# Windowed attention: score products of both heads ahead of their masks, and the next batch's products between scores and masks

## The reference, cut to what matters

```
L, D = 256, 256 in the block's own setup; here x is 1 x 1024 x 256
NQ, NKV, HD, SW = 32, 8, 64, 64;  QM = 4
q, k, v = split(layernorm(x) @ W_qkv);  q, k = rope(q), rope(k)
attn = einsum('bqhmd,bkhd->bhmqk', q, k) * sm_scale
mask = (q_pos >= k_pos) & (q_pos < k_pos + SW)
attn = where(mask, -inf, attn)
w = softmax(concat([attn, sink]))[..., :-1]
out = einsum('bhmqk,bkhd->bqhmd', w, v)
y = out @ W_out
```

## Time and profile before

| | |
|---|---|
| Runs of the kernel | 2770.3, 2771.74, 2782.01 us; median 2771.74 |
| Profiled execution | 2764.51 us, of which the span of the trace is 2762.8 |
| TensorE busy, whole span | 2515.4 us (91%) in 14474 products |
| VectorE, ScalarE, GpSimd busy | 1625.1 (59%), 1259.8 (46%), 1290.9 us (47%) |
| Second attention, from its first score tile | 634 to 1331 us of the span, 16 batches |
| In it, TensorE busy | 679.89 of 697.00 us |
| Mask products (L1836) | 288, 71.5 us busy, mean 248 ns |

### The profile page before, as it was taken

The page is one execution under the profiler, slowest core; times in us unless marked ns, Lnnn a source line. Parts: engine busy times, 40 slices in busy tenths (PEclk is TensorE's granted clock), DMA queues, the critical chain, the costliest instruction groups (busy, mean ns, idle before and its releaser), DMA issues. The chain is left out here.

```text
span 2762.8 us, 40694 instructions
## 1 busy us (share of the span) xinstructions
PE 2515.4 (91%) x14474; PEld 1675.7 (61%) x14474; DVE 1625.1 (59%) x2163; ACT 1259.8 (46%) x2174; POOL 1290.9 (47%) x1130
## 2 busy tenths in 40 slices
PE   6887999888999999999878878889999988998798
PEld 4443777654444444444564436678888877776676
DVE  4663555576766766665336543477777745555655
ACT  4464333464555555555434652256655643333322
POOL 4100344486888888888630002255454533442243
PEclk9798999998999999999976989899999999999899
DMA  1000111121101111010000001100010001110111
GB/s 59 1 2 11 39 46 46 48 80 39 39 16 39 31 31 39 16 35 1 25 26 1 1 1 49 47 20 28 20 32 20 20 5 42 46 46 21 31 41 43
DMA packets 39710, 81.63 MB, mean 30 GB/s; under 512 B 7553, under 2 KB 21121, under 8 KB 39041
## 3 DMA queue, kind: packets, MB, share of 16 engines
q1 hardware_dynamic: 39264, 79.41, 10.2%
q10 hardware_dynamic: 288, 0.13, 0.0%
HBM read 59.07 MB, written 2.62 MB: 22 GB/s over the span
## 5 line engine op out<-in xcount | busy, mean ns | idle before, releaser
L2019 DVE TENSOR_REDUCE a1h_mseg<-bank 128x2 f32<-128x1024 f32 x256 | 302.6, 1221 | 187.2 <-PE bank L1776 173.2
L63 POOL TENSOR_TENSOR f_wh<-f_raw,ones_r 128x768 fp32r<-128x768 f32 (+1 forms) x74 | 112.5, 1520 | 534.9 <-PE bank L462 360.0
L1953 ACT ACTIVATE a1h_prob<-bank 128x512 f32<-128x512 f32 x366 | 206.1, 598 | 165.6 <-PE bank L1836 83.8
L1756 POOL TENSOR_TENSOR a_qk<-a_qk,a1h_prob 128x512 f32<-128x512 f32 x186 | 238.9, 1318 | 50.8 <-ACT a1h_prob L1953 50.8
L451 PE MATMUL bank<-x_norm_h,f_wh 128*128 128x512 f32 x592 | 243.1, 411 | 6.7 <-PEq L3249 2.5
L451 PE MATMUL bank<-x_norm_l,f_wh 128*128 128x512 f32 x592 | 237.5, 401 | 0.0
L451 PE MATMUL bank<-x_norm_h,f_wl 128*128 128x512 f32 x592 | 237.0, 400 | 0.0
L658 DVE SCALAR_TENSOR_TENSOR f_tf<-bank,f_bias,f_sg 128x512 f32<-128x512 f32 x148 | 110.9, 750 | 187.2 <-PE bank L451 180.8
L542 ACT ACTIVATE f_hhi<-f_hf 128x512 fp32r<-128x512 f32 x124 | 78.3, 632 | 275.6 <-DVE f_hf L666 275.6
L1834 PE MATMUL bank<-a1h_ql,a1h_k 128*128 128x512 f32 x512 | 203.2, 397 | 0.0
L1849 PE MATMUL bank<-a1h_prob,a_v 128*64 128x512 f32 x732 | 179.9, 604 | 0.0
(11 more groups left out here) (597 smaller groups left out, 6277.1 us busy)
## 6 DMA issues: line engine op xcount, KB each, us to landing
f_raw<-in_l_w_dram SPq DMA_DIRECT2D x66, 385.0 KB, 3.0
a1h_st_q<-a_qk SPq DMA_DIRECT2D x128, 128.0 KB, 2.4
l2a_qkraw<-in_l2a_wqk_dram SPq DMA_DIRECT2D x32, 128.0 KB, 2.1
l2a_vraw<-in_l2a_wvg_dram SPq DMA_DIRECT2D x8, 512.0 KB, 3.7
f_raw<-in_l_w_dram SPq DMA_DIRECT2D x8, 449.0 KB, 3.3
a_qk<-l_keys SPq DMA_DIRECT2D x24, 128.0 KB, 2.7
a1p_raw<-in_l1a_w_dram SPq DMA_DIRECT2D x20, 128.0 KB, 2.1
a_qk<-in_l1a_wo_dram SPq DMA_DIRECT2D x16, 128.0 KB, 2.1
```

Source lines behind the costliest of these rows:

```text
L63: return pool.tensor_tensor(dst, src, one.to_broadcast(list(src.shape)), ALU.mult)
L1756: pool.tensor_tensor(out, first, slot_of[t % NP], ALU.add).then_inc(sum_done, 1)
L1953: act.activation(slot_of[t % NP], core.bank[2 + t % 3][:, :], ACT.Exp, scale=scale).then_inc(p_ready, 1)
L2019: dve.tensor_reduce(mseg[:, :, qb, s], spare(("A", n, k))[:, :, :], AX.X, ALU.max).then_inc(a_read, 1)
```

## The change

Only TensorE's order within a visit changes. `scores(n, i)` now does both heads of a step: the first head's two products, the second head's two, and without the masks. The masks of both heads follow in a function of their own, `mask_scores`. In the second step of a visit, where the next batch has segments in that visit and batch 0 isn't in its first three visits, the products of the two segments (`maxima`) go between that step's scores and its masks; the segments' masks come after the scores' masks. Everywhere else the masks follow the scores of their step at once. Every wait and every semaphore stays with its instruction, and no other engine's program is changed.

```diff
-            def scores(n, i, a):
+            def scores(n, i):
...
+                for a in range(PER):
...
+                    pe.matmul(bank[:, :], kn[:, G % 2, a, keys], QA[n % 2][:, a, half(h)], start=True, stop=False)
+                    mm = pe.matmul(bank[:, :], k1[:, a, keys], ql[:, n % 2, a, half(h)], start=False, stop=lo >= hi)
+                    if lo >= hi:
+                        mm.then_inc(s_ready, 1)
+            def mask_scores(n, i):
+
+                h, kb = TILES[i]
+                lo, hi = max(kb * P, h * HALF), min(kb * P + BAND, (h + 1) * HALF)
+                for a in range(PER if lo < hi else 0):
+                    bank = core.bank[2 + tile(n, i, a) % 3]
+                    pe.matmul(bank[:, lo - h * HALF:hi - h * HALF], core.ident_b[:, :],
+                              mk[:, 0, lo - kb * P:hi - kb * P], start=False, stop=True).then_inc(s_ready, 1)
...
                         for i in (2 * j, 2 * j + 1):
-                            scores(n, i, 0)
-                            scores(n, i, 1)
+                            scores(n, i)
+                            if i == 2 * j or (n == 0 and j < 3) or j == 7:
+                                mask_scores(n, i)
+                            else:
+                                for k in pairs[0:2]:
+                                    maxima(n + 1, k)
+                                mask_scores(n, i)
+                                for k in pairs[0:2]:
+                                    mask_maxima(n + 1, k)
...
-                        visit(n + 1, pairs[0:2])
+                        if (n == 0 and j < 3) or j == 7:
+                            visit(n + 1, pairs[0:2])
```

More of the change, by code:

```diff
@@ L1831, in scores @@
                 keys = slice(kb * P, (kb + 1) * P)
                 lo, hi = max(kb * P, h * HALF), min(kb * P + BAND, (h + 1) * HALF)
[L1833 to L1837, removed]
@@ L1838, in scores @@
-                mm.then_inc(s_ready, 1)
+                for a in range(PER):
+                    t = tile(n, i, a)
+                    bank = core.bank[2 + t % 3]
+                    if i == 0:
+                        pe.wait_ge(m_rows, rows_of(n) + a + 1)
+                        pe.wait_ge(q_lo, PER * n + a + 1)
+                    if n == 0 and i == TB:
+                        pe.wait_ge(m_rows, rows_of(n, "N") + a + 1)
+                    if i == 0 and a == 0:
+                        if n == 0:
+                            pe.wait_ge(k1_ones, PER)
+                        if n % 4 == 0:
+                            pe.wait_ge(k1_act, G + 1)
+                            pe.wait_ge(k1_dve, G + 1)
+                    if t >= 3:
+                        pe.wait_ge(p_ready, t - 2)
+                    pe.matmul(bank[:, :], kn[:, G % 2, a, keys], QA[n % 2][:, a, half(h)], start=True, stop=False)
+                    mm = pe.matmul(bank[:, :], k1[:, a, keys], ql[:, n % 2, a, half(h)], start=False, stop=lo >= hi)
+                    if lo >= hi:
+                        mm.then_inc(s_ready, 1)
```

## The result

The changed kernel is slower: median 2808.87 us of six runs (2799.57 to 2813.89), against 2771.02 for the kernel before (2761.31 to 2782.01, six runs). The ratio is 1.0121, 95% interval 1.0099 to 1.0144; of 2771 us that is 33.5 us, 27 to 40. The two medians lie 37.9 us apart, which is inside that interval.

The account below looks back on a forecast made before the run. TensorE's start-to-start product chain was taken as the bound. Visit costs over all batches summed to 36.1 us, less 1 given back: net +35 us, on the lowest run shown (2770.3) 2805 us; 8-in-10 range 2780 to 2820.

Parts of the forecast that it names:

- What bounds: Windowed attention: TensorE, busy 679.89 of 697.0 us, is near its limit; start-to-start distances count, not the weight path's 79.8 us idle.
- The new wait: Before the fourth K of masked visits: first tile's late mask, then its exponential, must finish; 0.77 us from mask end.
- fourth K: Fourth first score product (L1833) of a visit; in visit 6 forecast 2.06 us behind the first, against 1.79 before.
- Second mask behind the first: Score mask (L1836) directly behind another: starts 0.08 us later, bounds 0.03 and 0.24.
- M to m: From the next batch's row-maxima products (L1776) to the score masks (L1836): 0.67 us, type and tile shape both changing.
- The visits: Added time per masked visit: visits 1 and 6 +0.55 us, 0 +0.69, 5 +0.23, 7 +0.34; 2.36 a batch.
- V of visit 6: Start of visit 6's value products (L1849), counted from its first score product: forecast 3.85 us, against 3.30 before.
- The unmasked visits: Visits 2, 3, 4, order unchanged: said to run already at the exponential chain's limit, fourth K at 1.51 us.
- Given back: Masks now covering TensorE's waits for VectorE's reductions: under 1.9 us, taken as 1 us off the sum.
- (a): Rival: the wait before the fourth K doesn't bite, only tile shape changes cost; +12 us, 2783; chance 0.15.
- (b): Rival: no wait, mixing types was the cost, shape changes free between bf16 products; 8 us less, 2763; chance 0.12.
- (c): Rival: both added shape changes cost a full tail and load, 0.35 instead of 0.10; 29 us more, 2834; chance 0.07.

Follow-up runs that it names:

- grouped_only: Changed kernel, but the next batch's products stay behind all score masks; ratio to the kernel before 1.0102, stage 718.2 us (+22.0).
- odd_grouped: Kernel before, with both heads' masks together only in a visit's second step (not visit 5), next batch's products behind them; ratio 0.9999, stage 692.8 us (-3.4).

## Why the prediction was right, point by point

- **What bounds.** TensorE's start-to-start chain did. The large idle figure of the weight path was no reserve: 34 us of it went (79.8 to 45.8) while the stage grew.
- **The new wait.** Forecast 0.77 from the end of the first mask to the fourth K. Measured 0.76: the mask at 910.49 ends 0.26 later, at 910.75, the K starts at 911.51. It makes the larger part, 22.0 us of the stage with the grouping alone.
- **Second mask behind the first.** I took 0.08 between bounds of 0.03 and 0.24. The pair is busy 0.34 where one is busy 0.26: 0.08.
- **M to m, type and shape at once.** I took 0.67; it is 0.66 (912.18 to 912.84). The last m to the row masks and these to V, 0.19 each: 913.12 - 912.84 = 0.28 for two masks (0.27 by my prices), 913.12 to 913.31 = 0.19.
- **The visits.** V of visit 6 at 3.87 against 3.85. The others in the timeline of TensorE, answering to the earlier trace rows:

```profile
875.91 0.50 PE L1835 MATMUL bank<-x_norm_l,a1h_kn 128*128 128x512 f32 x1 [0.20 <-DVE a1h_ql L2060]
...
879.25 1.94 PE L1857 MATMUL bank<-a1h_prob,a_v 128*64 128x512 f32 x8
...
904.39 0.48 PE L1835 MATMUL bank<-x_norm_l,a1h_kn 128*128 128x512 f32 x1
...
907.57 1.94 PE L1857 MATMUL bank<-a1h_prob,a_v 128*64 128x512 f32 x8
...
915.17 0.50 PE L1835 MATMUL bank<-x_norm_l,a1h_kn 128*128 128x512 f32 x1
...
918.04 0.44 PE L1809 MATMUL bank<-a1h_nident,a1h_mpos 128*64 128x128 f32 x4
```

  Visit 0, from its second K: 3.34 (forecast 3.36), visit 5: 3.18 (3.19), visit 7: 2.87 (2.85). A regular batch took 2.32 more, forecast 2.36.
- **The unmasked visits.** The prediction said that they run at the limit of the same chain, and took the fit of 0.77 to 0.01 us for evidence. The sum of the chain is right, but there it held only a weight load: with half the exponential the fourth K stayed at 1.50. That the chain's end and the K's own time fell together was chance.
- **Given back.** This term was mis-sized. I took 1 us, at most 1.9, for masks that cover a wait for a reduction; of the sum of 36.1 before it, 4.0 did not come. The three batches behind a change of keys took 0.32, 1.56 and 1.56 us less than the regular 2.32, 3.4 in all. Most of it is not the reduction's wait (6.4 us before, 5.2 after) but the copy's: its entry, three waits and 3.3 us before, is one wait of 1.2 after; the rest of it, 0.3 to 0.5 in each, was not traced. Batches 3, 7 and 11 took 0.8 of it back. Batch 0 also grew less than the 1.8 I gave it: from its first Q to `max_rows` for batch 1 it took 50.2 us before (635.0 to 685.23) and 51.0 after (637.8 to 688.80), 0.8 more. That it runs in part at a lower clock (0.52 granted from 635 to 640 us, 1.00 only from 656 on) and partly waits for VectorE was in the trace, and I had priced it like the others.
- **The rivals.** (a), no wait, is refuted by grouped_only and by the shortened exponentials. (b), faster, with it; a small part of its mechanism is true and shows in odd_grouped: 3.4 us where the grouping meets no wait. (c), dearer shape changes, is refuted by the visits: from M to the masks 0.66 where it needs 0.57 + 0.35, and taking that change away is worth 0.09. The Trainium skill states in "TensorEngine Tiling (Array Packing)", Tiling Modes, that a change of the tiling mode drains TensorE. What these traces show is a start about 0.1 us later at each change; that a drain is what takes this time, no run shows, and a full tail and weight load on top, as (c) read the rule, did not come.
- **The time.** 2805 forecast, 2808.87 measured. That these are only 3.9 us apart is partly luck: the stage grew by 2.9 less than the net sum, and the medians by 5.8 more than the stage. The errors of the scale (the run's level, 14.5 us in the profiled execution outside the stage) are larger than those of the sum.

## What to carry to other kernels

Before reordering products for the sake of types or weight loads, look which buffer of the ring the next tiles take over, and add up the chain from the last write of its old tile: here 0.12 + 0.60 + 0.05 us had a slack of 0.19, and the reordering wrote that tile's end 0.46 later. Idle time of the weight path is not idle time of the array; read costs from start to start. Work of another tile shape, put into a group to keep types together, costs two shape changes, here about 0.1 us each.

## What the runs showed that I had not expected

The same copy on VectorE, 64 x 1024 values from SBUF to SBUF, takes 0.69 us in one order of events and 1.72 in the other. Before, GpSimd's sum had started at 992.87 and takes 1.28, the copy was started at 992.99 and ended at 994.71, 0.56 behind the sum's end at 994.15. After, the copy starts at 1012.93 and takes 0.69, and it is the sum whose length grows: it starts 0.03 behind the copy and takes 1.80 where 1.28 is usual.

```profile
992.87 1.28 POOL L1756 TENSOR_TENSOR a_qk<-a_qk,a1h_prob 128x512 f32<-128x512 f32 x1
```

```profile
1012.96 1.80 POOL L1756 TENSOR_TENSOR a_qk<-a_qk,a1h_prob 128x512 f32<-128x512 f32 x1
```

So a shift of 0.15 us (the copy 0.12 behind the sum's start, or 0.03 ahead of it) decides who waits for whom, and a copy of 0.7 us can cost 1.0 more on the path of TensorE. The Trainium skill ("SBUF — State Buffer", Who interferes with whom) states that VectorE and GpSimd share a pair of ports as an exclusive lock, that a cast on VectorE can take it in a two-port mode, and that whichever instruction comes later is blocked for the whole of the first. The trace agrees, but for 0.13 us: before, the copy ends 0.56 behind the sum's end, 0.13 less than its 0.69 alone; after, the sum ends 1.14 behind the copy's end (1014.76 against 1013.62), 0.14 less than its 1.28. That it is the ports which the two contend for rests on the page; no run separates them from another shared thing. It is also why "given back" could hardly be read from the kernel before alone: its order doesn't tell which of the two comes first once everything has shifted.
